# Gathers and scatters of a routed feed-forward tail: issued in two runs, and issued in turns

## The chip, the cores and the metric

The kernel runs on one core of a Trainium2 chip. The metric is the device time of one launch in microseconds. A profiled execution gives the span from the first to the last instruction and the trace that is read below.

## What is computed

The reference takes x of 8 x 1024 rows of 256 floats and applies three residual blocks: half a feed-forward block, a causal attention with a relative-position bias, and the feed-forward block again with the same weights. Each feed-forward block is a small attention, a layer norm, and a mixture of eight experts with a capacity of 1024 rows each:

```python
slot = jnp.where(keep, idx.astype(jnp.int32) * cap + loc, E * cap)
disp = jnp.zeros((E * cap, D), x.dtype).at[slot].set(xf, mode='drop')
h = jnp.einsum('ecd,edf->ecf', disp, w1) + b1[:, None, :]
y = (jnp.einsum('ecf,efd->ecd', h, w2) + b2[:, None, :]).reshape(E * cap, D)
out = jnp.where(keep[:, None], gate_val[:, None] * y[jnp.minimum(slot, E * cap - 1)], 0.0)
y2 = _ln(y1 + _moe(y1, wg, w1, b1, w2, b2), ln2_g, ln2_b)
```

There is no activation between the two expert matrices, so the kernel multiplies them into one 256x256 matrix per expert.

## The kernel before, in words

The function `ffn` runs twice, as `ffn1` (`turn` 0) and `ffn2` (`turn` 1). It has two parts. The first, `ffn_attention`, goes over the rows in order and writes to a DRAM tensor `rows` two things per row, side by side: the normalised row and the residual with the second norm's shift added, together 2 KB. The second part is called the tail here. The change is in the tail alone.

The tail begins when VectorE has written `inv` (L1435): for each of the 8192 expert slots, the number of the row that belongs there. The slots are worked on in 16 groups (`NG`) of four tiles (`GT`) of 128 rows; two groups belong to one expert. All 16 groups have their own place in the SBUF tensor `xs`, so no group waits for another's space, save in `turn` 0, where groups 10 to 15 lie where the expert matrices are (waits at L1103 to L1107).

GpSimd's queue holds, in this order: the gathers of groups 0 to 15, four indirect DMAs each (L1094), 128 rows of 2 KB per DMA; then the scatters of groups 0 to 15, four indirect DMAs each (L1112), 128 rows of 1 KB per DMA, into the block's output. Gather n first waits until gather n-2 has landed (`got`). Scatter n first waits for `s_fin` to reach n + 1. At the end GpSimd waits for all scatters to land.

The other engines run a pipeline with the order written out by hand. The first two and last two groups are unrolled, those between run in a hardware loop (`groups`, L116):

```python
# ScalarE, body(n), L1211            # TensorE, body(n), L1336
place(n + 2); xT_out(n + 1)          transposes(n + 1)
seeds(n + 1); root(n)                products(n)
normalise(n - 1)
# VectorE, body(n), L1503
sums(n); factors(n - 1); scale(n - 2)
```

`place` (L1153) waits for the gather of its group and copies the rows to `y1`. `transposes` (L1234) turns them, `xT_out` (L1160) copies them from PSUM, `seeds` (L1166) puts the expert's bias into PSUM, `products` (L1329) multiplies by the expert's matrix in two halves. `sums` (L1466 to L1485) adds the gated product to the gathered row and takes the norm's statistics, its second half being a second pair of L1472. `root` (L1171) and `factors` (L1491, L1493) make the norm's factors, `normalise` (L1176) applies them, and `scale(n)` (L1498, L1501), called in VectorE's body n + 2, multiplies by the gain, adds the second half of the row and raises `s_fin` to n + 1.

In `turn` 0 the expert matrices are also made while the gathers run: TensorE turns w1 (L1246), multiplies by w2 (`product(e)`, L1257), and sums biases (L1288), and VectorE makes the bias products (`bias_product`, L1448 and L1451) and adds them (L1439). The pipeline of groups begins behind the last of these, after `bias_sum(7)`.

The diff touches these lines:

Of the kernel before, what the change touches and what calls it, by code (L numbers as in the profile page):

```python
# [22 lines left out]
B, T, C = 8, 1024, 256  # L23
# [3 lines left out]
GT = 4  # L27
GW = GT * P
NG = TILES // GT
# [913 lines left out]
def ffn(core, name, x, rows, d, w12d, b12d, out, turn, tables):  # L943
# [4 lines left out]
    FB = FF // P  # L948
    CT = TILES // NG * 2
    MINE = (2, 5)  # L950
    with Phase(core, name) as ph:
        logits = ph.sb("logits", [P, TILES, NE])

        def tile(n, *shape, dt=F32):
            return ph.sb(n, [P, *shape], dt)
        mx, se, first, keep, loc, rank, drop, dscan, t2, t3 = (tile(n, TILES) for n in (
            "mx", "se", "first", "keep", "loc", "rank", "drop", "dscan", "t2", "t3"))
        xs = ph.sb("xs", [P, NG, GT, 2 * C])
# [3 lines left out]
        def lent(k, *shape):  # L962
# [25 lines left out]
        inv, gates = tile("inv", TILES, dt=U32), tile("gates", TILES)  # L988
# [17 lines left out]
        s_got, s_sent = core.indirect[0:2], core.indirect[2]  # L1006
        got0, sent0 = turn * 16 * TILES // 2, turn * 16 * TILES
        s_tps, s_tsb, s_zps, s_sum, s_st, s_mv, s_ve, s_sd, s_inv2, s_rs, s_norm, s_scaled, s_fin, s_marked, s_seed = (
            ph.sem(x) for x in ("tps", "tsb", "zps", "sum", "st", "mv", "ve", "sd", "inv2", "rs", "norm", "scaled", "fin",
                                "marked", "seed"))  # L1010
# [8 lines left out]
        def got(eng, n, u):  # L1019

            eng.wait_ge(s_got[u], (n - u) * (8 * GT) + got0 + 16 * GT)
# [40 lines left out]
        @block.sync  # L1062
        def _(sp):
            attend_sync(sp)
            if turn == 0:
                for e in range(2, 5):
                    load_w1(sp, e)
                for e in range(4, NE):
                    load_w2(sp, e)
                    if e + 1 < NE:  # L1070
                        load_w1(sp, e + 1)
                sp.wait_ge(s_w12sb, NE)
                sp.dma_start(w12d, w12[:, :, :].rearrange("p k c -> p (k c)")).then_inc(s_kept, 16)
                sp.wait_ge(s_b12sb, NE)
                sp.dma_start(b12d, b12[:, :]).then_inc(s_kept, 16)
                sp.wait_ge(s_kept, 32)
            else:
                over_yet(sp)
                sp.dma_start(w12[:, :, :].rearrange("p k c -> p (k c)"), w12d).then_inc(s_w, 16)

        @block.gpsimd
        def _(pool):
            nc.gpsimd.iota(ei[:, :], pattern=[[1, NE]], base=0, channel_multiplier=0).then_inc(s_iota, 1)
            nc.gpsimd.iota(ib[:, :], pattern=[[1, P]], base=0, channel_multiplier=0).then_inc(s_ib, 1)
            nc.gpsimd.iota(ni[:, :], pattern=[[1, TILES]], base=0, channel_multiplier=TILES).then_inc(s_ni, 1)
            nc.gpsimd.memset(zero[:, :], 0.0).then_inc(s_zero, 1)
            attend_gpsimd(pool)

            def gather(n):
                if n >= 2:  # L1090
                    got(pool, n - 2, n % 2)
                for t in range(GT):
                    i = n * GT + t
                    pool.indirect_dma_start(xs[:, n, t, :], None, rows,  # L1094
                                            bass.IndirectOffsetOnAxis(ap=inv[:, i:i + 1], axis=0)
                                            ).then_inc(s_got[n % 2], 16)

            for u in range(2):
                stored(pool, u)
            pool.wait_ge(s_inv, 1)  # L1100
            for n in range(NG):
                if turn == 0 and n in (10, 11):
                    pool.wait_ge(s_etps, 4 * (n - 3))  # L1103
                if turn == 0 and n >= 12:
                    pool.wait_ge(s_w12ps, n - 7)
                    pool.wait_ge(s_acc, n - 7)
                gather(n)  # L1107
            for n in range(NG):
                pool.wait_ge(s_fin, n + 1)
                for t in range(GT):  # L1110
                    i = n * GT + t
                    pool.indirect_dma_start(out, bass.IndirectOffsetOnAxis(ap=inv[:, i:i + 1], axis=0),  # L1112
                                            xs[:, n, t, 0:C], None).then_inc(s_sent, 16)
            pool.wait_ge(s_sent, sent0 + 16 * TILES)

        @block.scalar
        def _(act):
# [17 lines left out]
            def scaled(lo, hi):  # L1135
                act.wait_ge(s_zero, 1)
                for q in range(lo, hi):
                    if q in MINE:
                        continue
# [85 lines left out]
        def _(pe):  # L1225
# [45 lines left out]
            def inverse():  # L1271
                for q in range(CHUNKS):
                    pe.wait_ge(s_onm, q + 1)
                    if q in MINE:
                        pe.wait_ge(s_mine, MINE.index(q) + 1)
                    else:
                        pe.wait_ge(s_ong, q + 1 - sum(m < q for m in MINE))
                    for k in range(CT):
# [64 lines left out]
        def _(dve):  # L1343
# [76 lines left out]
            for q in range(CHUNKS):  # L1420
# [7 lines left out]
                                ALU.mult).then_inc(s_onm, 1)  # L1428
                if q in MINE:
                    dve.wait_ge(s_onm, q + 1)  # L1430
# [991 lines left out]
def macaron(nc, d, out):  # L2422
    def scratch(name, shape, dt=F32):
        return nc.dram_tensor(name, shape, dt, kind="Internal").ap()

    x = d["L0_attn_x"].rearrange("b t c -> (b t) c")
    y = out.rearrange("b t c -> (b t) c")
    x1, x2 = (scratch(n, (S, C)) for n in ("x1", "x2"))
    rows = scratch("rows", (S, 2 * C))
    w12d, b12d = scratch("w12d", (P, KB * NE * C)), scratch("b12d", (P, NE * C))  # L2430
    qd, kd = (scratch(n, (B * C, 3, T), BF16) for n in ("qparts", "kparts"))
    relrow = scratch("relrow", (AH, 2, 3 * P))
    neard = scratch("neard", (AH, P, PITCH))
    neardT = scratch("neardT", (AH, P, PITCH))
    lowd = scratch("lowd", (2 * B * NHG, LOW_PARTS, HG * T // 2), BF16)
    with ExitStack() as ctx:
        core = Core(nc, ctx)
        prepare(core, d, relrow)
        ffn(core, "ffn1", x, rows, d, w12d, b12d, x1, 0, distance_tables(relrow, neard, neardT))
        with Phase(core, "attention") as ph:  # L2440
            vall = ph.sb("vall", [P, B * NHG, QB, HG * AD])
            attention_qkv(core, x1, qd, kd, vall)
            attention_core(core, qd, kd, neard, neardT, lowd, vall)
            attention_out(core, x1, vall, x2)
        ffn(core, "ffn2", x2, rows, d, w12d, b12d, y, 1, ())
# [27 lines left out]
```

## Time and profile before

| | us |
|---|---|
| runs of the kernel, median of 3 | 2800.32 |
| lowest and highest | 2793.59, 2802.80 |
| the profiled execution, its time | 2796.27 |
| its span | 2794.5 |
| TensorE matmul busy | 2350.3 (84%) |
| VectorE busy | 2150.2 (77%) |
| ScalarE busy | 1657.6 (59%) |
| GpSimd busy | 818.8 (29%) |
| gathers L1094, x128 | 122.8 busy |
| scatters L1112, 2 x 64 | 65.2 + 65.2 busy |

Busy times are sums over instructions; an engine that waits is not busy. The first tail's gathers and scatters lie at 540 to 767 us of the span, the second tail's at 2577 to 2788. "Issue" as the cause of idle time means that the profile shows nothing that the engine waited for, and "remote" that it waited for a semaphore whose setter the profile does not name. PEclk is the granted TensorE clock, 1.00 for 2.4 GHz and 0.50 for 1.2 GHz.

### The profile page before, as it was taken

Reading aid. Unit: us, or ns where it says so; the run is one execution under the profiler, and the core shown is the slowest. Engines: PE = TensorE matmul, PEld = TensorE weight load, DVE = VectorE, ACT = ScalarE, POOL = GpSimd, SP = SyncE. Lnnn points to the kernel's source line nnn. Section 1 sums busy time; section 2 is a strip of 40 time slices with the busy share of each in tenths; the row PEclk is TensorE's granted clock in tenths of the full one; section 3 lists DMA queues with packets and bytes.
Section 4 is the critical chain, followed back from the end, with each engine's and each line's share of the span. In section 5 each row is a group of like instructions: output and inputs, shape, how many; then the busy total and the mean of one; then the engine's idle time right before and its main releaser. Section 6 shows DMA issues by size and latency. Waiting matters only on the chain. (4 is left out here: it accounts for less than half of the span.)

```text
span 2794.5 us, 47798 instructions
## 1 busy us (share of the span) xinstructions
PE 2350.3 (84%) x15864; PEld 1424.9 (51%) x15864; DVE 2150.2 (77%) x5653; ACT 1657.6 (59%) x3995; POOL 818.8 (29%) x853
## 2 busy tenths in 40 slices
PE   5999998867479969999999999999869999984263
PEld 4666665746345514444444444444646666663243
DVE  5888887727778869888898988997448888886076
ACT  3455453416534429999999999999215545442154
POOL 2243443263634420000000000000223344331735
PEclk8999999878789969999999999999989999996677
DMA  4132213382235464454554544542441121111712
GB/s 119 53 98 73 69 56 134 133 259 94 79 128 172 160 130 102 93 109 99 101 109 91 105 104 96 111 94 44 139 140 54 46 69 53 61 52 55 210 62 73
DMA packets 244680, 281.50 MB, mean 101 GB/s; under 512 B 41809, under 2 KB 212881, under 8 KB 243809
## 3 DMA queue, kind: packets, MB, share of 16 engines
q1 hardware_dynamic: 218192, 218.81, 30.7%
q0 software_dynamic: 16384, 50.35, 5.7%
q10 hardware_dynamic: 9872, 9.45, 1.0%
q8 instruction: 123, 2.02, 0.3%
q14 instruction: 109, 0.88, 0.1%
HBM read 190.63 MB, written 94.16 MB: 102 GB/s over the span
## 5 line engine op out<-in xcount | busy, mean ns | idle before, releaser
L2208 DVE CUSTOM_DVE_ANT_0 banks<-banks,attn_bias 128x128 f32<-128x128 f32 (+7 forms) x1024 | 759.9, 778 | 109.1 <-PE banks L1917 83.3
L2121 ACT ACTIVATE attn_probT<-banks 128x512 f32<-128x512 f32 x1152 | 622.6, 621 | 61.7 <-PE banks L1934 51.4
L1917 PE MATMUL banks<-attn_kst,attn_qst 96*128 96x512 bf16 (+3 forms) x1536 | 421.9, 336 | 22.9 <-DMA attn_kst<-kparts 12.7
L1934 PE MATMUL banks<-attn_qst,attn_kst 99*128 99x256 bf16 (+3 forms) x2176 | 410.8, 281 | 15.0 <-ACT attn_probT L2121 6.8
L1956 PE MATMUL banks<-attn_probT,attn_vb 128*32 128x256 f32 (+3 forms) x4352 | 316.0, 400 | 7.7 <-ACT attn_probT L2121 7.3
L1934 PEld LDWEIGHTS banks<-attn_qst,attn_kst 99*128 99x128 bf16 x2176 | 187.8, 98 | 168.5 <-ACT attn_probT L2121 54.5
L2266 POOL CAST attn_lowp<-attn_lowT 128x32 bf16<-128x32 f32 x64 | 13.4, 209 | 851.4 <-DVE attn_lowT L2216 851.4
L421 PE MATMUL banks<-ffn_xT,winT 128*128 128x512 f32 x512 | 250.9, 613 | 6.0 <-ACT ffn_w L621 2.9
L1917 PEld LDWEIGHTS banks<-attn_kst,attn_qst 96*128 96x128 bf16 x1536 | 117.5, 97 | 257.3 <-DVE attn_low L2208 159.2
L2109 ACT COPY banks<-attn_biasT 128x512 f32<-128x512 f32 x384 | 227.8, 628 | 28.3 <-DMA attn_biasT<-neardT 21.7
L881 POOL TENSOR_TENSOR ffn_xs<-ffn_xs,row_ffn_out 128x1024 f32<-128x1024 f32 x32 | 75.3, 2354 | 413.6 <-DVE ffn_xs L763 387.1
L591 ACT ACTIVATE ffn_xs<-banks,ffn_xs 128x128 f32<-128x128 f32 x512 | 182.4, 379 | 13.0 <-DVE ffn_xs L728 11.6
L1956 PEld LDWEIGHTS banks<-attn_probT,attn_vb 128*32 128x32 f32 x4352 | 106.2, 109 | 132.8 <-ACT attn_probT L2121 69.9
L630 ACT COPY ffn_xs<-banks 128x256 f32<-128x256 f32 x128 | 48.2, 377 | 203.6 <-PE banks L470 200.2
L1329 PE MATMUL banks<-ffn_w,ffn_xT 128*128 (+1 forms) x512 | 135.0, 419 | 40.3 <-issue 30.3
L1094 POOL DMA_INDIRECT ffn_xs<-rows,ffn_inv x128 | 122.8, 960 | 146.8 <-DVE ffn_inv L1435 94.1
L621 ACT ACTIVATE ffn_w<-banks,ffn_qk_b 64x512 f32<-64x512 f32 x128 | 87.3, 682 | 128.7 <-PE banks L421 127.9
L728 DVE TENSOR_REDUCE ffn_xs<-banks 128x4 f32<-128x512 f32 x128 | 88.5, 691 | 89.7 <-PE banks L450 89.7
L450 PEld LDWEIGHTS banks<-ffn_w,ffn_xs 128*128 128x128 f32 x1024 | 133.8, 198 | 23.7 <-issue 20.3
L450 PE MATMUL banks<-ffn_w,ffn_xs 128*128 128x128 f32 x1024 | 143.6, 285 | 0.8 <-DVE ffn_xs L750 0.8
L2208 DVE DVE_READ_ACCUMULATOR2_ANT attn_low<- 128x1 f32 x1024 | 144.3, 141 | 0.0
L736 DVE TENSOR_SCALAR ffn_xs<-ffn_xs 128x128 f32<-128x128 f32 x512 | 137.8, 331 | 4.5
(254 smaller groups left out, 4489.5 us busy)
## 6 DMA issues: line engine op xcount, KB each, us to landing
rows<-ffn_xs SPq DMA_DIRECT2D x64, 512.0 KB, 3.1
attn_qst<-qparts SPq DMA_DIRECT2D x384, 64.0 KB, 2.8
attn_kst<-kparts SPq DMA_DIRECT2D x192, 128.0 KB, 4.9
ffn_xs<-in_L_ffn_w_dram SPq DMA_DIRECT2D x16, 1024.0 KB
attn_biasT<-neardT SPq DMA_DIRECT2D x128, 128.0 KB, 4.9
attn_bias<-neard SPq DMA_DIRECT2D x128, 128.0 KB, 2.2
qparts<-qkv_part SPq DMA_DIRECT2D x32, 384.0 KB, 2.8
kparts<-qkv_part SPq DMA_DIRECT2D x32, 384.0 KB, 2.8
```

Of the source, the lines that this page charges most:

```text
L421: mm = nc.tensor.matmul(bank[QK], core.winT[:, k, j * P:(j + 1) * P], xT[:, u, k, :], start=(k == 0), stop=(k == KB - 1))
L450: mm = nc.tensor.matmul(bank[SC[t % 2]][:, h * P:(h + 1) * P], qT[:, u, h // 2, t * P:(t + 1) * P], kT[:, u, h, t * P:(t + 1) * P], start= ...
L591: ins = nc.scalar.activation(prob[:, t % 2, h, :], bank[SC[t % 2]][:, h * P:(h + 1) * P], ACT.Exp, bias=negm[:, t % 2, h:h + 1], scale=1.0 ...
L736: ins = nc.vector.tensor_scalar(prob[:, t % 2, h, :], prob[:, t % 2, h, :], rinv[:, t % 2, h:h + 1], None, ALU.mult)
L1094: pool.indirect_dma_start(xs[:, n, t, :], None, rows, bass.IndirectOffsetOnAxis(ap=inv[:, i:i + 1], axis=0)).then_inc(s_got[n % 2], 16)
L1329: mm = nc.tensor.matmul(part, xT[:, u, k, t * P:(t + 1) * P], w12[:, k, expert(n, u)], start=False, stop=(k == KB - 1), skip_group_check=True)
L1917: mm = nc.tensor.matmul(score[k % 2][:, a:e], qst[0:K6, u, half, hh, ii * P:(ii + 1) * P], kst[0:K6, u, hh, a:e], start=True, stop=True)
L1934: mm = nc.tensor.matmul(tbank[t % 3][:, at:at + nb * P], kst[:, u, hh, j * P:(j + 1) * P], qst[:, u, half, hh, x:x + nb * P], start=(k == ...
L1956: mm = nc.tensor.matmul(obank[32 * hh:32 * hh + 32, x:x + nb * P], vb[:, u, j, hh, :], probT[:, g % 2, i, at:at + nb * P], start=hh not in ...
L2109: nc.scalar.copy(tbank[t % 3].rearrange("p (a c) -> p a c", a=2), over(near[:, 0:2 * P], 2, 1)).then_inc(s_seed, 1)
L2121: nc.scalar.activation(probT[:, g % 2, i, 0:w], tbank[t % 3][:, 0:w], ACT.Exp, scale=-1.0).then_inc(s_exp, 1)
L2208: nc.vector.tensor_tensor_reduce(out=part, in0=part, in1=bias[:, hh, T - w:T], scale=1.0, scalar=BIG, op0=ALU.add, op1=ALU.min, accum_out= ...
```

## The change

GpSimd's queue in both tails gets another order. The gathers of groups 0 to 3 come first. Then, for n from 4 to 15, the gather of group n is followed by the scatter of group n - 4 with its wait for `s_fin`. The scatters of groups 12 to 15 come last. Waits, semaphores, sizes and the other engines' programs stay as they are.

```diff
@@ -948,6 +948,7 @@
     MINE = (2, 5)
+    LEAD = 4
@@ -1095,6 +1096,13 @@
+            def scatter(n):
+                pool.wait_ge(s_fin, n + 1)
+                for t in range(GT):
+                    i = n * GT + t
+                    pool.indirect_dma_start(out, bass.IndirectOffsetOnAxis(ap=inv[:, i:i + 1], axis=0),
+                                            xs[:, n, t, 0:C], None).then_inc(s_sent, 16)
+
@@ -1105,12 +1113,10 @@
                     pool.wait_ge(s_acc, n - 7)
                 gather(n)
-            for n in range(NG):
-                pool.wait_ge(s_fin, n + 1)
-                for t in range(GT):
-                    i = n * GT + t
-                    pool.indirect_dma_start(out, bass.IndirectOffsetOnAxis(ap=inv[:, i:i + 1], axis=0),
-                                            xs[:, n, t, 0:C], None).then_inc(s_sent, 16)
+                if n >= LEAD:
+                    scatter(n - LEAD)
+            for n in range(NG - LEAD, NG):
+                scatter(n)
             pool.wait_ge(s_sent, sent0 + 16 * TILES)
```

## Rows read from the trace of the kernel before

**Rows 1.** Windows: PE, PEld, DVE, ACT, POOL busy (instructions), PEclk, DMA share, GB/s.
```profile
2577.70:2602.60 24.90, 15.80 (x63) 11.99 (x62) 0.22 (x1) 8.50 (x12) 19.05 (x20) 0.79 0.68 192
2602.60:2657.60 55.00, 7.47 (x21) 5.09 (x20) 3.76 (x13) 3.32 (x6) 41.59 (x44) 0.56 0.73 210
2657.60:2678.50 20.90, 7.57 (x22) 5.28 (x22) 10.62 (x34) 8.00 (x16) 0.00 (x0) 0.52 0.07 23
2678.50:2764.50 86.00, 62.53 (x289) 49.75 (x287) 77.09 (x218) 60.51 (x119) 47.63 (x48) 0.94 0.20 72
571.00:602.00 31.00, 17.04 (x53) 10.43 (x52) 4.09 (x9) 1.17 (x2) 22.77 (x25) 0.62 0.84 267
```
**Rows 2.** Groups by line, GpSimd: busy us, mean ns, idle before and its causes.
```profile
L1112 POOL DMA_INDIRECT out_dram<-ffn_xs,ffn_inv x64 | 65.2, 1019 | 64.3 <-DVE ffn_xs L1501 49.0 <-issue 15.2
```
**Rows 3.** Timeline, second tail, GpSimd: start, us, line, op, count, idle before.
```profile
2581.66 0.95 POOL L1094 DMA_INDIRECT ffn_xs<-rows,ffn_inv  x1 [0.30 <-issue]
...
2601.65 0.94 POOL L1094 DMA_INDIRECT ffn_xs<-rows,ffn_inv  x1 [0.30 <-issue]
...
2656.65 0.95 POOL L1094 DMA_INDIRECT ffn_xs<-rows,ffn_inv  x1 [0.30 <-issue]
2678.54 1.00 POOL L1112 DMA_INDIRECT out_dram<-ffn_xs,ffn_inv  x1 [20.95 <-DVE ffn_xs L1501]
...
2686.83 0.97 POOL L1112 DMA_INDIRECT out_dram<-ffn_xs,ffn_inv  x1 [3.45 <-DVE ffn_xs L1501]
...
2764.54 0.96 POOL L1112 DMA_INDIRECT out_dram<-ffn_xs,ffn_inv  x1 [0.69 <-DVE ffn_xs L1501]
...
2786.10 0.97 POOL L1112 DMA_INDIRECT out_dram<-ffn_xs,ffn_inv  x1 [0.30 <-issue]
```
**Rows 4.** Timeline, second tail, VectorE, second half of `sums(0)`.
```profile
2622.60 0.88 DVE L1472 SCALAR_TENSOR_TENSOR ffn_xs<-banks,ffn_gnow,ffn_xs 128x256 f32<-128x256 f32 x2 [19.10 <-issue]
```
**Rows 5.** Timeline, first tail, GpSimd.
```profile
606.73 0.94 POOL L1094 DMA_INDIRECT ffn_xs<-rows,ffn_inv  x1 [4.72 <-remote]
...
659.19 1.01 POOL L1112 DMA_INDIRECT x<-ffn_xs,ffn_inv  x1 [22.78 <-DVE ffn_xs L1501]
...
741.29 1.99 POOL L1112 DMA_INDIRECT x<-ffn_xs,ffn_inv  x1 [0.30 <-issue]
...
765.52 0.97 POOL L1112 DMA_INDIRECT x<-ffn_xs,ffn_inv  x1 [0.30 <-issue]
```
**Rows 6.** Timeline, first tail, TensorE while the expert matrices are made.
```profile
568.53 7.07 PE L1257 MATMUL banks<-ffn_xs,ffn_xT 128*128 128x256 f32 x32
577.28 1.35 PE L1246 MATMUL banks<-ident,ffn_xs 128*128 128x128 f32 x8 [1.68 <-issue]
...
604.21 7.11 PE L1257 MATMUL banks<-ffn_xs,ffn_y 128*128 128x256 f32 x18 [0.82 <-issue]
...
631.45 1.19 PE L1288 MATMUL banks<-ffn_acc,ones 128*128 128x256 f32 x2 [3.05 <-DVE ffn_b L1439]
```
**Rows 7.** Timeline, second tail, ScalarE, `place` of groups 0, 3 and 4.
```profile
2585.49 1.04 ACT L1153 COPY ffn_y<-ffn_xs 128x1024 f32<-128x1024 f32 x1 [2.51 <-DMA ffn_xs<-rows,ffn_inv]
...
2625.74 1.03 ACT L1153 COPY ffn_y<-ffn_xs 128x1024 f32<-128x1024 f32 x1
...
2672.69 1.03 ACT L1153 COPY ffn_y<-ffn_xs 128x1024 f32 x1
```
**Rows 8.** Timeline, first tail, ScalarE, `place` of group 3.
```profile
646.25 1.03 ACT L1153 COPY ffn_y<-ffn_xs 128x1024 f32<-128x1024 f32 x1
```
**Rows 9.** Timeline, first tail, VectorE: last bias product, and a `scale`.
```profile
627.36 3.61 DVE L1451 SCALAR_TENSOR_TENSOR ffn_acc<-ffn_xs,b1T,ffn_acc 128x256 f32<-128x256 f32 x7
...
741.22 1.22 DVE L1498 TENSOR_TENSOR ffn_xs<-ffn_xs,row_ln_g 128x1024 f32<-128x1024 f32 x1
```
**Rows 10.** Timeline, second tail, TensorE, products of groups 2 and 3.
```profile
2646.22 3.77 PE L1329 MATMUL banks<-ffn_w,ffn_xT 128*128 x8 [17.35 <-issue]
...
2675.61 4.74 PE L1329 MATMUL banks<-ffn_w,ffn_xT 128*128 x16
```

## The prediction

> **What bounds the kernel now.** I read the windows of the two tails first, then GpSimd's timeline, then the rows of the engines it feeds. The second tail falls into stretches [rows 1]. From 2577.7 to 2602.6 us GpSimd issues 20 gathers and TensorE works (15.80 of 24.90 us). From 2602.6 to 2657.6 it issues the other 44, and everything else is nearly still: VectorE is busy 3.76 of 55.00 us, ScalarE 3.32. Then GpSimd waits 20.95 us for the first finished group. From 2678.5 to 2764.5 VectorE is busy 77.09 of 86.00 us. There it is the bound: twelve groups in 86.0 us, 7.17 us each. GpSimd's scatters, 1.019 us each and 0.30 apart inside a group [rows 2], follow it at 4 x 1.27 = 5.1 us per group. The last issue begins at 2786.10 and ends at 2787.07 [rows 3].
>
> The silence in the middle is no data wait. The second half of the first `sums` starts after 19.10 us of idle with no releaser [rows 4]. The matching stretch of the first tail, 571.0 to 602.0, shows the same, VectorE busy 4.09 of 31.00 us [rows 1]. It ends where GpSimd itself pauses: its last gather before the pause ends at 602.0 (606.73 less 4.72) [rows 5], and from 604.21 TensorE runs 18 matmuls in 7.11 us [rows 6]. I read this as: a long unbroken run of gathers starves the other engines of issue, and a pause of about 2 us frees them. The rows don't show through what.
>
> **The change, part by part.** No instruction is added or removed: 64 gathers and 64 scatters per tail, same sizes. Moved are eleven groups of scatters, each in front of a later gather group; scatter 11 only goes ahead of nothing. What is new is a wait: scatter m stands between gather m+4 and gather m+5 and waits for `s_fin`. Behind it on GpSimd's queue are all later gathers.
>
> (a) *Gain: the silence.* Up to gather 4's last issue, ending 2602.59 [rows 3], nothing differs. Then GpSimd waits for group 0, so the starvation should end about 2.1 us later: the second half of `sums` starts at 2604.7 in place of 2622.60. From there to ScalarE's `place(3)` is 3.14 us (2622.60 to 2625.74) [rows 4, 7]. From a `place` to the scatter it ends up releasing is 12.94 us in the first tail (646.25 to 659.19) [rows 5, 8] and 14.14 us in the second (2672.69 to 2686.83) [rows 3, 7]; I take their mean here, 13.5. Scatter 0 begins at 2604.7 + 3.1 + 13.5 = 2621.3 instead of 2678.54, 57.2 us earlier.
>
> First tail: gather 4 ends at 571.0 there. What stands between `product(5)` and the last bias sum is TensorE's own work once starvation is gone: 568.53 + 7.07, transposes from 577.28 for about 2.0, `product(6)` and `product(7)` of 7.07 each with three bias sums of about 0.6 before and between, then VectorE's last bias product of some 4.0 us (3.61 for seven of its eight steps) and 0.5 of handovers: 577.3 + 2.0 + 14.1 + 1.8 + 4.0 + 0.5 = 599.7 against 631.45 [rows 6, 9]. So scatter 0 begins 31.7 us earlier, at 627.5 instead of 659.19 [rows 5].
>
> (b) *Price: LEAD is one group short.* Scatter m needs `scale(m)`. VectorE does that after `sums(m+2)`, which needs `xT_out(m+2)`, and ScalarE issues that behind `place(m+3)`. So scatter m hangs on the landing of gather m+3, the group issued just before scatter m-1 and gather m+4. From the end of a gather group's issue to its `place` are 2.88 us (2582.61 to 2585.49) [rows 3, 7]. With 14.14 that is L = 17.0 us from the end of gather m+3 to the start of scatter m; with 12.94 it is 15.8. I take 17.0: TensorE had idled before that one (clock 0.52 in that stretch [rows 1]), as it will before every group now. GpSimd gets back to scatter m after 5.1 us of scatters and 5.0 of gathers (16 issues in 19.99 us, 2581.66 to 2601.65) [rows 3], so 10.1. It is too early, and waits. Going round twice, two groups take L + 10.1 = 27.1 us, 13.6 per group, where VectorE needed 7.17.
>
> Written out from scatter 0 (S0): gather 5 ends at S0 + 10.1; ten more gather groups take 5 x (L + 10.1); scatter 12 starts L behind gather 15. From there to GpSimd's last issue 22.5 us as before (2764.54 to 2787.07) [rows 3]. Sum: S0 + 83.1 + 6L = S0 + 185.1 us. Before, it was 108.5 us from scatter 0 in the second tail and 107.3 in the first (659.19 to 766.49) [rows 3, 5].
>
> (c) *Collision.* Gathers will now run beside VectorE's long additions, where they had an idle VectorE. One scatter of the first tail took 1.99 us instead of 0.97; it began at 741.29, VectorE's 128x1024 multiplication at 741.22 [rows 5, 9]. Bounds are none and one such stretch (1.02 us) per pair of groups, six per tail, 6.1 us. In the old steady part scatters start just after these operations and escape; I take half, 3.1 us per tail. The Trainium skill (SBUF — State Buffer, "SBUF: two separate sides") says GpSimd and a VectorE operation that holds the shared port pair block each other fully, and that descriptor writing counts. By that rule I would take all six, 6 us more in the total; the row above agrees with it.
>
> Landing and the waits inside `gather` (`got`, and in the first tail `s_etps`, `s_w12ps`, `s_acc`) cost nothing: each is for something more than one pair of groups old. What follows GpSimd's last issue (7.4 us to the span's end) stays.
>
> **Sum.** Second tail: last issue ends at 2621.3 + 185.1 + 3.1 = 2809.5, against 2787.07: +22.4. First tail: 627.5 + 188.2 = 815.7 against 766.49: +49.2. Together +71.6 us on the profiled execution's 2796.27 makes 2867.9. The median of the shown runs is 4.1 above that execution and they spread over 9.2, so I add half the difference: 2870 us.
>
> Ends: L = 15.8, no stretch and S0 2 and 6 us earlier (release at once in each tail) give +37, about 2838 with the median's offset. Upper: TensorE at 1.2 GHz through every product: 8 matmuls took 3.77 us in the slow stretch, so 16 take 7.5 against 4.74 [rows 10], L = 19.8, and six stretches: +111, but then scatter 0's gain also stays; I cut this to 2905, because even the restart shown took 4.74.
>
> **Rivals.** *GpSimd's issue is the bound (faster).* If landing to finish were hidden, L at most 10.1, the formula gives S0 + 143.7: second tail 2765.0 (-22), first 771.2 (+5), total 2779 us. The place is the wait in scatter m; the two tails break even with before when 2 x (83.1 + 6L) = 304.8, at L = 11.6. For: 10.1 us per group would still feed most of it, and 89 us of early start are to be had. Against: 15.8 and 17.0 are both measured, in two tails. Chance 0.07.
>
> *Equal within 0.3%* (about what a measurement of this kernel can tell from no change): L of 11 to 12, or pairs overlapping in a way I missed. 0.04.
>
> *Starvation stays (slower still).* In each pair of groups GpSimd now issues 16 DMAs without a break, gathers and scatters mixed, and before, TensorE ran through the first 16 to 20 gathers. If the silence does not end at the pause, up to 57 + 32 us come back: 2959. For: in the old second tail TensorE was still slow after the gathers ended, 7.57 us busy of 20.90 [rows 1]. Against: the restart in the first tail. 0.07.
>
> *The forecast*, alternate waits of about 7 us, has 0.82. The change does what it says only in form: GpSimd takes turns, but the gathers stop being ahead.
>
> Range: 2838 to 2905 leaves out both side cases and the extremes of L. Chances: faster 0.08, same 0.04, slower 0.88.
>
> **What would show it.** Scatter 0 near 2621 in the second tail (plus what the first tail shifted) and at 627 in the first. Then GpSimd's idle before scatters alternating, about 7 us before each even one and nearly none before the odd, released by `scale` (L1501 before the change). VectorE's busy share between scatter 0 and 12 falls from 0.90 to about 0.5, TensorE's clock with it. ScalarE's `place` waits on the gathers' landing throughout. I am wrong if `place` finds its group landed (then L is hidden), if GpSimd never waits after scatter 0, or if VectorE stays silent past 575 in the first tail.

## The result, and the profile after the change

| | before | after |
|---|---|---|
| median us (runs) | 2801.48 (4) | 2870.51 (4) |
| lowest and highest | 2793.59, 2802.80 | 2861.19, 2876.03 |
| profiled execution, its span | 2796.27, 2794.5 | 2861.19, 2859.5 |
| first gather to end of last issue, tail 1 | 225.8 | 274.5 |
| the same, tail 2 | 209.3 | 230.4 |

The ratio of the times is 1.0249, 95% interval 1.0213 to 1.0285: slower, as forecast. Forecast were 2870 us and tails longer by 49.2 and 22.4 us; they are longer by 48.7 and 21.1. The table counts one execution of the kernel before more than the table ahead of the change. Its lower two lines are differences of timeline rows, as 2855.26 - 2624.89.

GpSimd's timeline in the second tail after the change (columns as in [rows 3]; L1095 is the gather, L1103 the scatter):

```profile
2669.77 1.00 POOL L1103 DMA_INDIRECT out_dram<-ffn_xs,ffn_inv  x1 [20.03 <-DVE ffn_xs L1507]
...
2678.95 0.95 POOL L1095 DMA_INDIRECT ffn_xs<-rows,ffn_inv  x1 [0.30 <-issue]
2680.21 1.00 POOL L1103 DMA_INDIRECT out_dram<-ffn_xs,ffn_inv  x1 [0.30 <-issue]
...
2689.16 0.95 POOL L1095 DMA_INDIRECT ffn_xs<-rows,ffn_inv  x1 [0.30 <-issue]
2696.87 1.00 POOL L1103 DMA_INDIRECT out_dram<-ffn_xs,ffn_inv  x1 [6.76 <-DVE ffn_xs L1507]
...
2704.57 1.43 POOL L1095 DMA_INDIRECT ffn_xs<-rows,ffn_inv  x1 [0.30 <-issue]
2706.30 1.11 POOL L1095 DMA_INDIRECT ffn_xs<-rows,ffn_inv  x1 [0.30 <-issue]
...
2724.03 1.00 POOL L1103 DMA_INDIRECT out_dram<-ffn_xs,ffn_inv  x1 [6.42 <-DVE ffn_xs L1507]
...
2832.73 0.97 POOL L1103 DMA_INDIRECT out_dram<-ffn_xs,ffn_inv  x1 [10.63 <-DVE ffn_xs L1507]
...
2854.29 0.97 POOL L1103 DMA_INDIRECT out_dram<-ffn_xs,ffn_inv  x1 [0.30 <-issue]
```

Read the brackets. Scatter 0 waited 20.03 us. Scatter 1 (2680.21) waited for nothing, scatter 2 (2696.87) 6.76 us, scatter 4 (2724.03) 6.42. So it goes on: a wait before each even scatter, almost none before the odd ones. Where those waits come from stands on ScalarE, in its `place` of groups 5 and 6:

```profile
2683.04 1.04 ACT L1159 COPY ffn_y<-ffn_xs 128x1024 f32 x1 [14.03 <-DMA ffn_xs<-rows,ffn_inv]
2693.03 1.04 ACT L1159 COPY ffn_y<-ffn_xs 128x1024 f32 x1 [4.87 <-DMA ffn_xs<-rows,ffn_inv]
```

Gather 5's last issue ends at 2679.90 (2678.95 + 0.95). Its `place` starts 3.14 us later, and scatter 2 another 13.83 us later. ScalarE now waits for landings, as this view of all waits between scatters 0 and 12 sums up (engine, target, line, releaser: sum of us, count, longest):

```profile
ACT ffn_y L1159 <- DMA ffn_xs<-rows,ffn_inv: 99.5, 11, 14.0
POOL out_dram L1103 <- DVE ffn_xs L1507: 52.3, 6, 20.0
```

The windows that answer to [rows 1] (same columns): the 20 gathers, the wait for group 0, scatters 0 to 12, the last three groups; last, scatters 0 to 12 of the first tail.

```profile
2624.80:2649.80 25.00, 15.62 (x62) 11.82 (x61) 0.00 (x0) 8.50 (x12) 19.06 (x20) 0.80 0.67 192
2649.80:2669.70 19.90, 11.41 (x50) 8.97 (x49) 14.48 (x49) 10.58 (x21) 0.00 (x0) 0.83 0.07 23
2669.70:2832.70 163.00, 70.06 (x280) 59.28 (x280) 78.96 (x217) 60.52 (x119) 93.87 (x92) 0.75 0.36 109
2832.70:2855.30 22.60, 0.00 (x0) 0.00 (x0) 11.10 (x23) 4.36 (x9) 17.41 (x16) 0.53 0.25 88
630.40:794.80 164.40, 73.33 (x280) 60.54 (x280) 79.24 (x217) 60.51 (x119) 93.54 (x92) 0.74 0.36 109
```

The 55.00 us of near-silence are gone. In exchange VectorE's twelve groups, 77.09 us of work in 86.0 before, are 78.96 us of work in 163.0. The same work is spread over nearly twice the time. The mean granted TensorE clock fell with it, from 0.94 to 0.75.

GpSimd's groups by line, against 122.8 us and 960 ns for the gathers and 65.2 us, 1019 ns for each 64 scatters before [rows 2]:

```profile
L1095 POOL DMA_INDIRECT ffn_xs<-rows,ffn_inv x128 | 131.8, 1030 | 136.3 <-DVE ffn_inv L1441 94.1 <-issue 37.8 <-DMA ffn_xs<-rows,ffn_inv 4.4
L1103 POOL DMA_INDIRECT x<-ffn_xs,ffn_inv x64 | 64.6, 1009 | 120.8 <-DVE ffn_xs L1507 103.6 <-issue 17.2
L1103 POOL DMA_INDIRECT out_dram<-ffn_xs,ffn_inv x64 | 64.5, 1008 | 80.8 <-DVE ffn_xs L1507 63.6 <-issue 17.2
```

### The profile page after: what moved, and what is told of

Same layout as the page of the kernel before. It is cut to its first block and busy times, and to the rows that moved or that the text cites. A ratio compares the mean times of both kernels' runs of the same rounds, so it can differ in the third digit from the quotient of the medians.

```text
span 2859.5 us, 47798 instructions
## 1 busy us (share of the span) xinstructions
PE 2353.2 (82%) x15864; PEld 1441.5 (50%) x15864; DVE 2158.0 (75%) x5653; ACT 1656.0 (58%) x3995; POOL 829.2 (29%) x853
## 5 line engine op out<-in xcount | busy, mean ns | idle before, releaser
L1240 PE MATMUL banks<-ident,ffn_y 128*128 128x128 f32 x256 | 54.9, 385 | 195.2 <-ACT ffn_y L1159 164.7
L1095 POOL DMA_INDIRECT ffn_xs<-rows,ffn_inv x128 | 131.8, 1030 | 136.3 <-DVE ffn_inv L1441 94.1
L1159 ACT COPY ffn_y<-ffn_xs 128x1024 f32 (+1 forms) x32 | 33.3, 1043 | 209.7 <-DMA ffn_xs<-rows,ffn_inv 209.7
L1240 PEld LDWEIGHTS banks<-ident,ffn_y 128*128 128x128 f32 x256 | 44.1, 200 | 208.0 <-issue 175.4
```

Source lines behind the costliest of these rows:

```text
L1095: pool.indirect_dma_start(xs[:, n, t, :], None, rows, bass.IndirectOffsetOnAxis(ap=inv[:, i:i + 1], axis=0)).then_inc(s_got[n % 2], 16)
L1240: mm = nc.tensor.transpose(bank[2 * u + k][:, t * P:(t + 1) * P], y1[:, u, t, k * P:(k + 1) * P], core.ident[:, :])
```

## The experiments

Two statements were to be tested. The first: the loss is L, the latency from landing to finish, which a lead of four groups does not cover. The second: a long run of indirect DMAs without a break starves the other engines of issue. The rivals: the landing or the queues of the DMA engines set the alternating wait, and it is the bytes moved that silence the engines. A kernel with half the bytes in each gather, which would have varied the bytes alone, gave no result. Each kernel is compared with the kernel before on the same chip. That matters here, since the kernel before takes about 2801 us on some chips and about 2730 on others. The first three ran on a chip where it takes 2798.58.

**Five groups of lead.**

```diff
-    LEAD = 4
+    LEAD = 5
```

> The changed kernel with LEAD 5 in place of 4, nothing else. Theory A (program order: scatter m hangs on the landing of gather m+3, L = 17 us after that group's issue ends, and with LEAD 4 GpSimd is back after 10.1 us): with LEAD 5 it is back after 20.2 us, more than 17, so it stops waiting in the steady part and its own issues bound, 10.1 to 10.5 us per group in place of 13.7. From scatter 0 to GpSimd's last issue about 141 to 146 us in place of 186; scatter 0 some 4 us later than with LEAD 4. Each tail about 36 to 42 us shorter than with LEAD 4: total 2785 to 2798 us, at or just under the kernel before. Theory B (mixing gathers and scatters on one DMA queue delays the landing): the waits stay whatever the lead, 13 us per group, total about 2865.

Measured: 2843.64 us (2840.53 to 2846.93), ratio 1.0163 (1.0146 to 1.0180). The tails are 261.9 and 225.7 us long. Better than LEAD 4, but far from what was expected. The alternating wait is gone, and another has come: every third group of scatters waits about 9 us, one 10.6. GpSimd, TensorE and VectorE around one of them, and the window of the last gathers before it:

```profile
2686.70 0.99 POOL L1095 DMA_INDIRECT ffn_xs<-rows,ffn_inv  x1 [0.30 <-issue]
...
2700.53 1.00 POOL L1103 DMA_INDIRECT out_dram<-ffn_xs,ffn_inv  x1 [9.06 <-DVE ffn_xs L1507]
```
```profile
2676.09 4.82 PE L1335 MATMUL banks<-ffn_w,ffn_xT 128*128 x16
```
```profile
2681.58 0.17 DVE L1472 COPY ffn_gnow<-ffn_gates 128x4 f32 x1 [7.51 <-PE banks L1335]
...
2694.24 0.88 DVE L1478 SCALAR_TENSOR_TENSOR ffn_xs<-banks,ffn_gnow,ffn_xs 128x256 f32 x2 [11.42 <-remote]
```
```profile
2682.80:2691.40 8.60, 5.90 (x24) 5.17 (x24) 0.03 (x1) 3.03 (x5) 6.71 (x7) 0.80 0.48 144
```

The products ended at 2680.91, yet the second half of `sums` starts only at 2694.24. For 11.42 us VectorE did nothing, and the profile names no setter of what it waited for. TensorE and ScalarE still worked at that time (5.90 and 3.03 of 8.60 us); VectorE came back about 3 us after the last gather of the run. I read it as the stall of [rows 4], shorter and on one engine, at the end of a run of 24 DMAs. It is no wait for code to be loaded: between 2651 and 2816 us the queues that carry instructions show no packet. With the alternating wait removed the run grew from 16 to 24, and starvation came back.

**Program order of ScalarE and TensorE**, at LEAD 4.

```diff
-                if not ends(n, 2):
-                    place(n + 2, u)
                 if not ends(n, 1):
...
                     seeds(n + 1, 1 - u)
+                if not ends(n, 2):
+                    place(n + 2, u)
                 root(n, u)
...
+                products(n, u)
                 if not ends(n, 1):
                     transposes(n + 1, 1 - u)
-                products(n, u)
```

> The changed kernel, GpSimd's queue untouched with LEAD 4, but ScalarE's body calls place(n+2) behind xT_out(n+1) and seeds(n+1), and TensorE's body calls products(n) ahead of transposes(n+1). Then sums(m+2) hangs on gather m+2 and no longer on gather m+3. Theory A: GpSimd has 20.2 us from the end of gather m+2 to scatter m and needs about 17, so its waits in the steady part vanish: 10.1 to 10.5 us per group, each tail 40 us shorter, total about 2780 to 2795. If the reordered pipeline has a longer chain of its own (transposes behind products, about 1 to 4 us more) a wait of up to 2 us per pair of groups may stay, total up to 2805. Theory B (queue contention): nothing of this kind, total 2855 to 2880.

Measured: 2850.94 us (2844.26 to 2858.21), ratio 1.0185 (1.0160 to 1.0209), tails 269.7 and 222.9. The DMAs and their queues are the same as after the change, but the regular 7 us before every even scatter are gone. So that wait hung on the order of work, `xT_out(m+2)` behind `place(m+3)`, and not on the queues. (Scatter m still hangs on gather m+3, since `root(m+1)` and `normalise(m)` stay behind `place(m+3)`, but by a shorter chain.) In its place GpSimd waits as at LEAD 5: in the first tail before every third group, 9.1, 10.4 and 9.1 us, again after 24 DMAs without a break. In the second tail the waits are less regular, behind silences of VectorE of 3 to 12 us. The first of them there:

```profile
2710.61 1.00 POOL L1103 DMA_INDIRECT out_dram<-ffn_xs,ffn_inv  x1 [9.04 <-DVE ffn_xs L1507]
```

I had expected both kernels below 2805 us. I had taken for granted that starvation stays away once GpSimd no longer has all 64 gathers in one run.

**The order of before, with a break after each gather group.** Gather n waits until gather n-1 has landed.

```diff
-                if n >= 2:
-                    got(pool, n - 2, n % 2)
+                if n >= 1:
+                    got(pool, n - 1, (n - 1) % 2)
```

> The kernel before, all gathers ahead of all scatters, but gather n waits for gather n-1 to land in place of n-2, so that GpSimd makes a break of about 2.9 us after every four gathers. Theory S1 (an unbroken run of gathers starves the other engines of issue and a short break frees them): the other engines' silence is gone from both tails, VectorE runs its groups at the gathers' 7.9 us pace, gathers end about 126 us after they began, and 64 scatters follow without a wait in 82 us: second tail 0 to -5 us, first tail about -15 to -20, total 2775 to 2790. Theory S2 (bytes in flight or gathers of any kind beside the pipeline starve it, breaks or not): the silence stays, VectorE busy under 0.2 for 50 us and more, and the gathers, now slower, push everything out: 2830 or more.

Measured: 2808.55 us (2797.02 to 2821.05), ratio 1.0036 (1.0020 to 1.0052), a miss again. The windows of the second tail: the gathers, then two pieces of the scatters.

```profile
2582.70:2707.20 124.50, 81.70 (x347) 63.18 (x346) 78.31 (x227) 69.62 (x131) 66.52 (x64) 0.86 0.47 132
...
2722.00:2737.00 15.00, 5.19 (x16) 4.04 (x16) 0.00 (x0) 1.59 (x3) 11.39 (x12) 0.69 0.29 105
2737.00:2752.00 15.00, 0.00 (x0) 0.00 (x0) 1.05 (x3) 0.00 (x0) 11.34 (x13) 0.54 0.28 100
```
```profile
2737.63 0.17 DVE L1466 COPY ffn_gnow<-ffn_gates 128x4 f32<-128x4 f32 x1 [17.79 <-remote]
```

During the gathers the cure works: VectorE is busy 78.31 of 124.50 us. Then 64 scatters come without a break, and they starve VectorE as the gathers did, 0.00 of 15.00 us. They do so at 100 to 105 GB/s and a DMA share of 0.28, where the silence of before had 210 GB/s and 0.73 [rows 1]. So it needs neither a high rate of bytes nor gathers. In the old order the scatters wait for VectorE after every four, and I take those waits to have been their breaks; that was not tested by itself.

The length of the run does not decide it alone. In the first tail of the same trace the last four gathers and all 64 scatters follow one another without a break too, from 678.4 us on, and VectorE works through until its last group is done at 721:

```profile
683.80:700.00 16.20, 11.57 (x52) 9.09 (x52) 14.35 (x44) 11.10 (x23) 12.83 (x12) 0.91 0.33 112
700.00:720.00 20.00, 5.55 (x24) 4.22 (x22) 18.75 (x44) 10.14 (x22) 15.43 (x16) 0.76 0.26 93
```

That is some 32 DMAs without a silence, where in the second tail it began after 14. No run here shows what made the difference.

**Three ways to break the run.** These ran on one chip, where the kernel before takes 2728.82 us. The first puts a short instruction of GpSimd's own behind each group, at LEAD 5:

```diff
+                nc.gpsimd.memset(ei[:, :], 0).then_inc(s_brk, 1)
+                pool.wait_ge(s_brk, breaks[0])
```

> LEAD 5, and after every group of four indirect DMAs GpSimd writes one small tile (128x8) and waits for that write itself, a break of some tenths of a us. Theory S3 (an unbroken run of indirect DMAs on GpSimd, gathers or scatters, starves the others' issue after about 16 to 20 of them; any break resets it): the 9 to 11 us waits of every third group seen with LEAD 5 vanish, 10.4 to 11 us per group, total 2785 to 2805. Theory S5 (the break has to be long enough for something to drain, about the 2 to 3 us of a landing): the tenths do nothing, the period of about 40 us per three groups stays, total 2840 to 2860.

The second, also at LEAD 5, waits for its own landing after every odd gather group:

```diff
                 gather(n)
+                if n % 2:
+                    got(pool, n, 1)
```

> LEAD 5, and after every second gather group GpSimd waits until that group has landed, about 2.9 us, so no run is longer than 16 indirect DMAs. Theory S3 or S5 alike: no silence of VectorE over 3 us after scatter 0, about 11.6 us per group (two groups 20.2 + 2.9), each tail about 15 to 20 us shorter than with LEAD 5 alone: total 2800 to 2820. If starvation does not depend on the length of the run but on the mean load, the silences stay: 2850 or more.

The third leads by nine groups in the first tail and six in the second:

```diff
+    LEAD = 6 if turn else 9
...
-                if n >= 2:
+                if 1 <= n <= LEAD:
+                    got(pool, n - 1, (n - 1) % 2)
+                elif n >= 2:
                     got(pool, n - 2, n % 2)
...
+                if n > LEAD and n % 2:
+                    got(pool, n, 1)
+                if n >= LEAD:
+                    scatter(n - LEAD)
...
+                scatter(n)
+                if n % 3 == 0 and n < NG - 2:
+                    pool.wait_ge(s_sent, sent0 + 64 * (n + 1))
```

> The lead is 9 groups in the first tail, where VectorE is late anyway, and 6 in the second; the gathers ahead of scatter 0 each wait for the one before to have landed; behind it every second gather group is followed by a wait for its landing, and among the last scatters every third group by a wait for the scatters to land. Theory S3 or S5: pipeline fed early and never starved; first tail's last issue about 12 us earlier than before, second tail's about 12 us earlier: total 2765 to 2785, faster than both kernels. If breaks of every 16 DMAs are too rare, a few silences of about 10 us stay: 2790 to 2810.

Measured: 2776.51, 2794.72 and 2781.51 us, ratios 1.0175 (1.0155 to 1.0195), 1.0245 (1.0228 to 1.0262) and 1.0195 (1.0178 to 1.0212). Once its pipeline has started, VectorE is never idle for over 7.3 us in any of them. The window between scatters 0 and 12 of the first:

```profile
2622.70:2748.10 125.40, 71.85 (x280) 59.33 (x279) 78.46 (x216) 59.32 (x118) 93.61 (x109) 0.81 0.43 134
```

GpSimd is busy 93.61 us there, and some 0.30 us before each of 109 instructions (88 DMAs and 21 of the small writes) is about 32 more: its issue is the bound, 125.4 / 12 = 10.4 us per group. With L hidden, that is the pace of my faster rival (10.1). All three are slower than the kernel before on this chip, though, and the runs that follow show a likely reason. They don't tell a cure from a chip that does not starve.

**Both kernels again, and short breaks in the old order**, on a chip where the kernel before takes 2801.21. The third kernel has the `memset` and its wait after each four DMAs, and nothing else changed:

> The kernel before itself, for its trace beside the others of this chip. Two chips have shown it at 2798.6 and at 2728.8 us. Theory C1 (the starvation of issue by an unbroken run of indirect DMAs is there on one chip and not on the other): a run near 2729 has no silence of VectorE during the gathers, tails of about 190 us each bound by GpSimd's 128 issues; a run near 2800 has both silences as in the trace already shown. Theory C2 (the chips differ elsewhere, in DMA or clock): the 70 us are spread over the phases.

> The changed kernel on the same chip as the run before. Theory C1: its own time hardly depends on the chip, because the 7 us waits for the finished group break the run of DMAs: about 2860 to 2870 on either chip, so 1.025 of before where before takes 2800, and 1.05 where before takes 2729. Theory C2: the ratio is 1.025 on both.

> The order of the kernel before, all gathers and then all scatters, with a break of some tenths of a us after every group of four indirect DMAs: one 128x8 write by GpSimd and a wait for it. Theory S3 (even a short break resets the starvation): no silence, scatters follow the gathers without a long wait, GpSimd's 128 issues and 31 breaks take about 170 us per tail: second tail -37 us and first tail about -30 us against the trace shown before, so 2725 to 2745 on either chip: -2.3% where before takes 2800, 0 to +0.5% where it takes 2729. Theory S5 (tenths are too short): 2800 on a chip where before takes 2800.

Measured: the kernel before 2802.72, with VectorE idle for 28.5, 19.8 and 36.4 us in its second tail (the first of these holds the start of the pipeline, 19.4 us on a chip without silences); the changed one 2874.17, ratio 1.0263 (1.0242 to 1.0283). The short breaks give 2803.25 (2798.82 to 2806.56), 1.0006 (0.9996 to 1.0016), and cure nothing:

```profile
2674.72 0.17 DVE L1477 COPY ffn_gnow<-ffn_gates 128x4 f32<-128x4 f32 x1 [40.45 <-remote]
```

They are hardly breaks, though. From the end of one gather (2590.96) to the start of the next they make 0.39 us where 0.30 is usual, so this test tells little about breaks between 0.4 and 1.7 us:

```profile
2590.01 0.95 POOL L1102 DMA_INDIRECT ffn_xs<-rows,ffn_inv  x1 [0.30 <-issue]
2590.96 0.12 POOL L1094 MEMSET ffn_ei<- 128x8 int32 x1
2591.35 0.95 POOL L1102 DMA_INDIRECT ffn_xs<-rows,ffn_inv  x1 [0.27 <-POOL ffn_ei L1094]
```

The changed kernel's trace here has a span of 2870.9 us, 11.4 more than the one shown above, with tails of 278.3 and 237.6 us. Some of its alternate waits are 3 us longer, up to 9.9 us. Group 6 in the second tail:

```profile
2718.06 4.32 PE L1335 MATMUL banks<-ffn_w,ffn_xT 128*128 x16
2721.34 0.95 POOL L1095 DMA_INDIRECT ffn_xs<-rows,ffn_inv  x1 [0.30 <-issue]
2724.30 0.17 DVE L1472 COPY ffn_gnow<-ffn_gates 128x4 f32 x1 [13.07 <-DMA ffn_xs<-rows,ffn_inv]
2731.85 1.00 POOL L1103 DMA_INDIRECT out_dram<-ffn_xs,ffn_inv  x1 [9.56 <-DVE ffn_xs L1507]
```

That group had landed long before (ScalarE placed group 7 at 2715.12), and all its products ended at 2722.38, but VectorE began with it only at 2724.30, 2.0 us after the last of 16 DMAs in a row. In the trace above it began 1.5 us before the products ended. So a run of 16 can already hold VectorE up, by some 3 us, in the changed kernel itself.

**A break of landing length after every eight DMAs, in the order of before**, and the kernel before beside it. This chip takes 2730.40 us for the kernel before.

```diff
                 gather(n)
+                if n % 2:
+                    got(pool, n, 1)
             for n in range(NG):
+                if n % 2 == 0 and n:
+                    pool.wait_ge(s_sent, sent0 + 64 * n)
                 pool.wait_ge(s_fin, n + 1)
```

> The order of the kernel before, with a break of landing length after every eight indirect DMAs: after every second gather group GpSimd waits for its landing (about 2.9 us), and before every second scatter group for the earlier scatters to land (about 1.7 us as seen among the last scatters of the hybrid). Theory S5 (a break has to last about as long as a landing takes, and eight DMAs between breaks are few enough): no silence; gathers 103 us, scatters about 94 us, 197 us per tail against 209 and 226: total 2765 to 2785 on a chip where before takes 2800, slower than before by about 40 us on a chip where it takes 2729. Theory S6 (breaks after eight are too rare, or scatters starve whatever breaks they have): VectorE silent again for 10 us and more during the scatters, 2800 or more.

> The kernel before, for its trace on this job's chip. Theory C1: if it takes 2729 us here, VectorE has no silence during the gathers and both tails are bound by GpSimd's issue at about 185 us each; if it takes 2800, the silences of 57 and 32 us are there as before. Theory C2: the difference between the chips lies outside the tails.

Measured: 2777.76 us (2775.28 to 2780.62), ratio 1.0177 (1.0160 to 1.0194), and for the kernel before 2731.39. The second tail of the kernel before, gathers and scatters, on this chip:

```profile
2550.30:2637.30 87.00, 62.17 (x283) 48.83 (x282) 60.44 (x178) 57.00 (x106) 67.51 (x65) 0.90 0.66 190
2637.30:2722.20 84.90, 25.80 (x110) 20.11 (x108) 42.43 (x112) 27.78 (x56) 65.69 (x64) 0.67 0.29 101
```
```profile
2637.30 1.00 POOL L1112 DMA_INDIRECT out_dram<-ffn_xs,ffn_inv  x1 [0.30 <-issue]
```

It is the same program, and at 190 GB/s it moves as much as the starved one, yet VectorE works through: 60.44 of 87.00 us while the gathers run. Scatter 0 waits for nothing, and 128 issues at about 1.34 us make up the whole tail of 171.9. After the start of the pipeline there (19.35 us of idle) VectorE is never idle for 7 us. This chip does not starve. Its tails are 195.3 and 171.9 us; on the chip of the run before they were 228.9 and 209.8. The difference is 71.5 us, and the spans differ by 71.4 (2801.0 and 2729.6). So the whole difference between these two executions lies in the tails, and I put it down to the starvation. Here the breaks only cost.

**The same kernel once more, on a chip that starves** (the kernel before takes 2801.86).

> The same kernel as the one with a break of landing length after every eight indirect DMAs, again, because the kernel before took 2730 us in its first job, where it has no silence to cure. If before takes 2800 here, theory S5 expects no silence of VectorE in either tail and about 2775, 0.99 of before; theory S6 expects silences of 10 us and more among the scatters and 2800 or more. If before takes 2729 here, 2777 and 1.018 again, and the question stays open.

Measured: 2775.92 us (2775.68 to 2777.18), ratio 0.9908 (0.9891 to 0.9925). Gathers and scatters of its second tail, and the first of its breaks among the scatters:

```profile
2563.90:2674.10 110.20, 78.44 (x349) 61.07 (x349) 76.78 (x227) 69.55 (x131) 68.53 (x65) 0.91 0.53 153
2674.10:2766.70 92.60, 10.72 (x43) 8.15 (x42) 25.84 (x62) 15.34 (x32) 63.59 (x64) 0.58 0.25 89
```
```profile
2698.80 0.97 POOL L1116 DMA_INDIRECT out_dram<-ffn_xs,ffn_inv  x1 [1.71 <-DMA out_dram<-ffn_xs,ffn_inv]
```

VectorE now does most of its work during the gathers, 76.78 of 110.20 us, and the scatters follow at GpSimd's pace. What is left of idle times of VectorE over 8 us is the start of the pipeline, 9.75 us in the first tail and 19.84 in the second, as without starvation (8.5 and 19.35). The breaks are 2.9 us and more after gathers and 1.7 among scatters. The tails are 214.1 and 202.8 us, against 228.9 and 209.8 above. It is 2776 to 2778 us on both kinds of chip: with the breaks the kind of chip no longer shows. On a chip that starves it is 0.9% faster than the kernel before. On the others the kernel before stays best of those tried. These breaks differ from the short ones in two ways, length and what they wait for, so it is not shown whether the time or the landing is the cure.

## Why the prediction was right

Step by step, in its own order.

(a) *Scatter 0.* The second tail's first gather starts 47.13 us later than before (2624.89 against 2577.76). Taken off, the second half of `sums(0)` starts at 2605.96, where 2604.7 was forecast:

```profile
2653.09 0.88 DVE L1478 SCALAR_TENSOR_TENSOR ffn_xs<-banks,ffn_gnow,ffn_xs 128x256 f32<-128x256 f32 x2 [0.33 <-PE banks L1335]
```

From there to scatter 0 it took 16.68 us, forecast 3.14 + 13.5. Scatter 0 is at 2622.6 so corrected, forecast 2621.3. In the first tail the first gather starts 2.31 later (542.96). The last bias sum and scatter 0, in that tail:

```profile
602.02 1.19 PE L1294 MATMUL banks<-ffn_acc,ones 128*128 128x256 f32 x2 [3.54 <-DVE ffn_b L1445]
```
```profile
630.44 1.01 POOL L1103 DMA_INDIRECT x<-ffn_xs,ffn_inv  x1 [58.24 <-DVE ffn_xs L1507]
```

Less 2.31 these are 599.7 and 628.1; 599.7 and 627.5 were forecast. So the engines worked on during the wait for group 0, the step for which the trace of before had least to show.

(b) *L.* Forecast 17.0; from gather 5 to scatter 2 it is 16.97, from gather 7 (2707.41) to scatter 4 16.6. Scatters 0, 2, 4, 6, 8 and 10 start 27.10, 27.16, 27.39, 27.33 and 27.41 us apart, where L + 10.1 = 27.1 and the collision were forecast. From scatter 0 to 12 are 163.0 us (2669.77 to 2832.73), forecast 60.6 + 102 + 3.1 = 165.7: L was 16.5 to 16.6 in the later pairs and 15.8 before scatter 12. Scatter 12 to the end of the last issue took 22.5, as forecast. The 17.0 was the nearer of the two measured latencies, for the reason given. TensorE, idle for 10.8 us before such a group, started it at a granted clock of 0.50: its eight transposes took 1.96 us and its sixteen products 4.44. In the first tail of before, where L would be 15.8, they took 1.09 and 3.72.

(c) *Collision.* The bounds were 0 and 6.1 us per tail, 3.1 taken. Gathers are 9.0 us dearer and scatters 1.3 cheaper over both tails (131.8 + 64.6 + 64.5 against 122.8 + 65.2 + 65.2), so 3.9 per tail. The form was not quite as forecast, not one stretch of 1.02 us per pair but two smaller ones. The gather at 2704.57 took 1.43 and ran beside this multiplication until 2705.18; the next, of 1.11 us, met the end of the addition that starts at 2705.37.

```profile
2703.95 1.23 DVE L1504 TENSOR_TENSOR ffn_xs<-ffn_xs,row_ln_g 128x1024 f32 x1
2705.37 1.22 DVE L1507 TENSOR_TENSOR ffn_xs<-ffn_xs  x1 [0.20 <-issue]
```

The first gather was stretched by 0.48 us over 0.61 us of overlap with the multiplication. The other four such gathers of this tail were stretched by 0.69 to 0.76 us over 0.82 to 0.89, and all five ended 0.82 us after the multiplication had. The Trainium skill (SBUF — State Buffer, "SBUF: two separate sides") describes an exclusive lock on a shared port pair, and GpSimd's side of the trace agrees with that. VectorE's side does not: the addition began while the gather ran and took its usual 1.22 us. Nor did the rule call for six stretches, as the prediction had it: the same section says that a `tensor_tensor` with both inputs in SBUF, which these two operations are, meets only GpSimd's reads and did not stall a DMA when it was probed. Here it did. It cost the overlap, not the length of the operation, and all six at 1.02 us would have been too much.

*Sum.* The tails gave +69.8 us, the span +65.0. The other 4.8 lie outside the tails: what lies between them is 3.9 us shorter (1811.3 to 1807.4), what follows the last issue 3.2 (7.4 to 4.2), what leads up to the first is 2.3 longer. I had left those as they were. That the median fell on 2870.51 is partly luck: the profiled execution is 6.7 us below its own sum of 2867.9 and the lowest of the four. What made the other three longer is not known; the later trace of 2870.9 us was longer by small silences of VectorE, a term that the sum had put at nothing.

Two slips in the working did not touch the forecast. By its own terms the lower end is +43 us (71.6 less 14.4, 6.2 and 8), about 2841, not +37 and 2838. And the 1.27 us per scatter is 0.97 + 0.30; the mean of 1.019 beside it includes stretched ones.

*The rivals.* The long silences did not stay at LEAD 4, where the waits of 7 us broke the run every 16 DMAs; what stayed, in the second of its traces, were delays of some 3 us. The two experiments that took this wait away brought silences of 7 to 12 us back. So the rival that ended slower was nearly wrong for this kernel and right for its next step. The faster rival needs L hidden and no starvation; its pace of 10 us per group was seen only on a chip that does not starve. There even the hybrid, the longest lead tried, was 1.0195 of the kernel before. With all gathers first, GpSimd never waits in the second tail on such a chip, so there taking turns can only add waits. In the first tail its scatters still wait 25.5 us for VectorE in all; none of the kernels tried won that back.

What stays open: through what the run of DMAs starves the others, what besides the length of the run decides, whether a break has to be long or has to see a landing, and what differs between the chips. Each chip was used in one sitting, so the chip and the sitting (the place of the tensors in memory, say) are not told apart. The changed kernel itself was not timed on a chip that does not starve. If its tails stayed 274.5 and 230.4 us there, it would be 138 us or 5% over the kernel before; that is an estimate.

## What to carry to other kernels

A lead is long enough only if (lead, less the groups that one group's result hangs on through every engine's program order) times the issue time per group covers the latency from landing to finish; here scatter m hung on gather m+3, so a lead of 4 left one group, 10.1 us against 17. When work is moved up in a queue, everything behind it inherits its wait. And a wait that is to be tuned away may be a break that something else lives on: ask what runs unbroken once it is gone.

## What the hardware showed that was not expected

- On some chips an unbroken run of indirect DMAs, at 1.3 us each, silenced the other engines, VectorE first: by some 3 us in some runs of 16, for 11.42 us in a run of 24, and for 17 to 40 us at a time around runs of 20 (the first tail of the kernel before) and of 56 and more, where TensorE and ScalarE stood nearly still too. It happened with gathers at 210 GB/s and with scatters at 100. Some 32 DMAs in a row also passed once without a silence.
- Waits for landings every eight DMAs (2.9 us and more among the gathers, 1.7 among the scatters) kept it away, ratio 0.9908. A gap of 0.39 us in place of 0.30 after every four did nothing (ratio 1.0006).
- It goes with the chip, or with the sitting. The medians of the kernel before were 2798.58 to 2801.86 us in four sets of runs and 2728.82 and 2730.40 in two, and between two traces, one of each kind, the tails alone made the difference, 71.5 of 71.4 us.
